# A macaron block on one core: routed experts run unmasked in one stream of tiles, and the choice of experts is multiplied in afterwards

## What is computed

```python
x = x + 0.5 * ffn(layernorm(x))
x = x + attention(layernorm(x))      # 16 heads of 8, 4 key heads, causal, ALiBi bias
x = x + 0.5 * ffn(layernorm(x))

def ffn(x):                           # 8 experts of 64, 2 chosen; one shared of 128
    scores = sigmoid(x @ gate_w.T + lb_bias)
    topw, topi = top_k(scores, 2)
    topw = topw / (topw.sum(-1) + 1e-8)
    for e in range(8):
        sel = (topi == e).any(-1)
        wmean = (topw * (topi == e)).sum() / max((topi == e).sum(), 1)
        y = (silu(x @ gate[e].T) * (x @ up[e].T)) @ down[e].T
        out += where(sel, y * wmean, 0)
    return out + shared_mlp(x)
```

## Time and profile before

| | us |
|---|---|
| median of 3 runs | 787.71 (786.26 to 789.75) |
| the profiled execution | 790.5, span 788.7 |
| PE busy | 733.0 (93% of the span) |
| DVE busy | 579.1 (73%) |
| ACT busy | 420.3 (53%) |
| POOL busy | 42.3 (5%) |
| mean granted TensorE clock | 0.961 |

### The profile page before, as it was taken

The page is one execution under the profiler, slowest core; times in us unless marked ns, Lnnn a source line. Parts: engine busy times, 40 slices in busy tenths (PEclk is TensorE's granted clock), DMA queues, the critical chain, the costliest instruction groups (busy, mean ns, idle before and its releaser), DMA issues.

```text
span 788.7 us, 15244 instructions
## 1 busy us (share of the span) xinstructions
PE 733.0 (93%) x5580; PEld 342.5 (43%) x5588; DVE 579.1 (73%) x1937; ACT 420.3 (53%) x610; POOL 42.3 (5%) x60
## 2 busy tenths in 40 slices
PE   5889998995899999999999999999998878899998
PEld 3634444553334444444444444444343466344443
DVE  5676332889899999999999999999994276643311
ACT  2433343332377776876777677777777523333211
POOL 3200000111000000000000000000000022000000
PEclk9799999996599999999999999999999988999999
DMA  7001000354100110101100110011000000000012
GB/s 204 1 0 16 0 0 1 118 161 137 56 19 24 32 36 21 30 23 36 31 24 19 37 36 19 20 36 36 20 19 1 2 1 1 0 1 0 1 40 67
DMA packets 37983, 26.15 MB, mean 33 GB/s; under 512 B 12026, under 2 KB 37242, under 8 KB 37908
## 3 DMA queue, kind: packets, MB, share of 16 engines
q1 hardware_dynamic: 37332, 25.09, 11.3%
q10 hardware_dynamic: 576, 0.08, 0.1%
HBM read 14.64 MB, written 10.26 MB: 32 GB/s over the span
## 4 chain that ended last, share of the span: by engine, by line
PE 48%; DVE 15%; issue 11%; ACT 2%; another core or an unknown queue 0%; DVEq 0%; ACTq 0%
PE ps L981 44%; DVE mx L866 8%; PE ps L986 4%; DVE mx L859 1%; ACT h_all L586 1%; DVE xn L665 1%; DVE stats L653 1%; DVE h_all L859 1%; DVE h_all L676 1%; DVE wb L886 0%; DVE mm_ L883 0%; DVE mv L657 0%; PE ps L1029 0%; ACT xnT_all L507 0%
## 5 line engine op out<-in xcount | busy, mean ns | idle before, releaser
L586 ACT ACTIVATE h_all<-ps 128x1024 f32<-128x1024 f32 (+3 forms) x384 | 291.2, 811 | 111.9 <-PE ps L981 108.7
L866 DVE TENSOR_REDUCE mx<-ps 128x1 f32<-128x512 f32 (+2 forms) x352 | 223.1, 681 | 10.2 <-PE ps L981 7.4
L981 PE MATMUL ps<-ks,xnT_all 57*128 57x512 bf16 (+3 forms) x768 | 179.2, 336 | 14.1 <-DVE mx L859 6.2
L981 PE MATMUL ps<-h_all,vb 128*32 128x512 f32 (+3 forms) x1536 | 163.9, 500 | 0.6 <-ACT osb L575 0.6
L981 PE MATMUL ps<-xnT_all,ks 59*128 59x512 bf16 (+3 forms) x768 | 158.2, 331 | 3.5 <-ACT h_all L586 3.4
L859 DVE CUSTOM_DVE_ANT_0 h_all<-ps,mask_w 128x384 bf16<-128x384 f32 (+1 forms) x256 | 149.3, 618 | 2.1 <-issue 0.5
L981 PEld LDWEIGHTS ps<-ks,xnT_all 57*128 57x128 bf16 x768 | 56.5, 94 | 144.4 <-DVE mx L859 64.7
L676 DVE TENSOR_TENSOR h_all<-ps,sg 128x512 f32<-128x512 f32 x80 | 54.9, 690 | 82.7 <-PE ps L981 51.4
L981 PE MATMUL ps<-cb 64*128 64x64 bf16 (+3 forms) x1216 | 112.5, 214 | 0.0
L503 ACT ACTIVATE sg<-ps 128x512 f32<-128x512 f32 x80 | 47.6, 597 | 101.3 <-PE ps L981 80.2
L981 PE MATMUL ps<-xnT_all,wg 128*128 128x512 f32 x160 | 88.8, 638 | 1.0 <-ACT sg L503 0.9
(11 more groups left out here) (119 smaller groups left out, 534.3 us busy)
## 6 DMA issues: line engine op xcount, KB each, us to landing
xnT_all<-q_scr SPq DMA_DIRECT2D x64, 96.0 KB
q_scr<-qp SPq DMA_DIRECT2D x8, 384.0 KB
ks<-k_scr SPq DMA_DIRECT2D x64, 48.0 KB
x<-in_x SPq DMA_DIRECT2D x8, 256.0 KB, 6.1
q_scr<-qp SPq DMA_DIRECT2D x8, 256.0 KB
out<-x SPq DMA_DIRECT2D x8, 256.0 KB, 2.3
k_scr<-kp SPq DMA_DIRECT2D x48, 32.0 KB
xnT_all<-bias_scr SPq DMA_DIRECT2D x64, 18.0 KB
```

The source lines that it names most:

```text
L586: act.activation(pr[:, (NSTEP * i + s) % PR_BUFS, p:HPG:SLOTS, lo:HALF], ps[:, b:b + 2, lo:HALF], ACT.Exp)\
L866: dve.tensor_reduce(m, src, AX.X, V.max).then_inc(a_out, 1)
L981: return pe.matmul(o, l, r, start=start, stop=stop, skip_group_check=True)
```

## The change

The routed tiles are no longer masked in the gate. All 40 tiles form one list, `TILE_ORDER`, group by group with the shared one first. Thirteen of them run inside the front (one behind the second turn, two behind each later one), 27 follow without a break. Within the front the logits of a group come one group later. The choice runs on DVE between the products of tiles 13 to 20; ahead of tile 20 PE turns the whole choice (128 tokens x 256 values, 0 or 1, bf16) with two transposes, and ACT copies it to `selT`. SP writes it to DRAM (`store_choice`, two DMAs, waited for) and reads it back for one group at a time (`load_mask`, two DMAs of 256 KB): each expert's row of 512 values goes to the 64 partitions of its hidden units. Two buffers hold these masks. POOL multiplies the routed part of `h_all` of a group with its mask, in place and in two halves of 128x1024 (`mask_hidden`, a semaphore `hm`); `down` waits for both.

In the first feed-forward POOL masks groups 0 to 3, then alternates: `rsqrt` c of the next norm, mask 4 + c, for c from 0 to 3, then `rsqrt` 4 to 7. SP loads masks 0 to 2 behind the choice, 3 to 5 behind the ALiBi rows and ACT's key copies, 6 and 7 behind the first stack. In the second feed-forward POOL masks all groups after its `rsqrt`s, and SP loads masks 6 and 7 among the stores of the output. The totals come ahead of tile 25 and the scaling of `wds` behind it; the slopes stand at tile 27, the eight ALiBi steps at tiles 28 to 35, one to a tile. The operands of the mask matmul (`esel`, `maskT`, `unsel`), their fills on POOL and one constant copy on ACT go away.

```diff
-LATE_SHARED = GROUPS - 4
+
+TILE_ORDER = [(c, i) for c in range(GROUPS) for i in (MT, *range(MT))]
+FRONT = (0, 1, 2, 2, 2, 2, 2, 2)
+FRONT_END = sum(FRONT)
+SEL_AT, TOPS_AT = FRONT_END + 7, FRONT_END + 12
+SLOPES_AT = FRONT_END + 14
+MASK_BUFS, MASK_PARTS = 2, 2
+AHEAD = GROUPS // 2
+
+
+def front_tiles(c):
+
+    return range(sum(FRONT[:c]), sum(FRONT[:c + 1]))
+
...
+            def store_choice(f):
+
+                sp.wait_ge(f.mk, 1)
+                rows = sel_scr.rearrange("e (a t p) -> a t e p", a=2, p=P)
+                for a in range(2):
+                    sp.dma_start(rows[a], selT[:, a, :]).then_inc(f.md, 16)
+                sp.wait_ge(f.md, 16 * 2)
+
+            def load_mask(f, c):
+
+                after(sp, f.hm, MASK_PARTS * (c - MASK_BUFS + 1))
+                rows = sel_scr.rearrange("(m k) n -> k m n", k=2)
+                for k in range(2):
+                    src = rows[k, None, :, c * GN:c * GN + GN].broadcast_to([INTER, MT, GN])
+                    sp.dma_start(expert_mask[c % MASK_BUFS][k * INTER:k * INTER + INTER], src)\
+                        .then_inc(s_mask[c % MASK_BUFS], 16)
+
+            store_choice(f1)
+            for c in range(AHEAD - 1):
+                load_mask(f1, c)
             sp.wait_ge(s_bst, 1)
             sp.dma_start(bias_scr[:, 0:2, :], bias_st[:, 0, None, :].broadcast_to([HEADS, 2, SEQ])).then_inc(s_bdma, 16)
...
+            for c in range(AHEAD - 1, AHEAD + 2):
+                load_mask(f1, c)
             store_parts(0, 0, 0)
             sp.wait_ge(f1.dw0, 16 * STORES)
             load_stack(0, 0, 0, 0)
+            for c in range(AHEAD + 2, GROUPS):
+                load_mask(f1, c)
             store_parts(1, 0, 1)
             sp.wait_ge(f1.dw1, 16 * STORES)
             load_stack(0, 0, 0, 1)
...
+            store_choice(f2)
+            for c in range(GROUPS - 2):
+                load_mask(f2, c)
             od = out.rearrange("(c t p) f -> c p t f", t=GT, p=P)
             for c in range(GROUPS):
+                if c < 2:
+                    load_mask(f2, GROUPS - 2 + c)
                 sp.wait_ge(f2.x, c + 1)
                 sp.dma_start(od[c], xt(c)).then_inc(f2.out, 16)
             sp.wait_ge(f2.out, 16 * GROUPS)
...
+            def mask_hidden(f, n, c):
+
+                uses = (n * GROUPS + c) // MASK_BUFS + 1
+                w = MT // MASK_PARTS
+                for part in range(MASK_PARTS):
+                    tiles = slice(w * part, w * part + w)
+                    pool.wait_ge(f.h, HT * c + 1 + w * part + w)
+                    if part == 0:
+                        pool.wait_ge(s_mask[c % MASK_BUFS], 32 * uses)
+                    pool.tensor_tensor(h_all[:, c, tiles, :], h_all[:, c, tiles, :], expert_mask[c % MASK_BUFS][:, tiles, :],
+                                       ALU.mult).then_inc(f.hm, 1)
+
             over_groups(lambda c, par, first, last: rsqrt(c, par, f1.ve, f1.xn, f1.rs))
             clear_keys()
-            pool.wait_ge(f1.U, HT * GROUPS)
-            over_groups(lambda c, par, first, last: rsqrt(c, par, f1.ve2, f1.xn2, f1.rs2))
+            pool.wait_ge(f1.xn, GROUPS)
+            for c in range(AHEAD):
+                mask_hidden(f1, 0, c)
+            for c in range(AHEAD):
+                rsqrt(c, c % 2, f1.ve2, f1.xn2, f1.rs2)
+                mask_hidden(f1, 0, AHEAD + c)
+            for c in range(AHEAD, GROUPS):
+                rsqrt(c, c % 2, f1.ve2, f1.xn2, f1.rs2)
 
             pool.wait_ge(s_late, 16 * len(late_loads))
...
+            for c in range(GROUPS):
+                mask_hidden(f2, 1, c)
...
+                    for k in front_tiles(c):
+                        silu(k, k % 2)
                     if load_constants and c == GROUPS - 2:
                         constants()
...
-                for c in range(LATE_SHARED, GROUPS):
-                    silu(c, c % 2)
-                mask_T(0, 0)
-                over_groups(routed_tiles)
+                for k in range(FRONT_END, len(TILE_ORDER)):
+                    if k == SEL_AT:
+                        act.wait_ge(f.mT, 1)
+                        act.activation(selT.rearrange("p a n -> p (a n)"), ps[:, 2, 0:P].bitcast(BF16), copy)\
+                           .then_inc(f.mk, 1)
+                    silu(k, k % 2)
...
+                    if not first:
+                        for k in front_tiles(c - 1):
+                            hidden(k)
...
+                def choose():
+                    later = iter(range(FRONT_END, len(TILE_ORDER)))
+
+                    def tile_between():
+                        hidden(next(later))
+
+                    dve.wait_ge(f.sig, 1)
+                    ch.link(dve.tensor_reduce(m1, sc, AX.X, V.max))
+                    ch.link(dve.tensor_tensor(eq, sc, wide(m1), V.is_equal))
                     ch.link(dve.tensor_tensor(eq, eq, rk, V.mult))
-                    ch.link(dve.tensor_reduce(r, eq, AX.X, V.max))
-                    ch.link(dve.tensor_tensor(sel, rk, wide(r), V.is_equal))
-
...
+                    tile_between()
+                    ch.link(dve.tensor_reduce(r1, eq, AX.X, V.max))
+                    ch.link(dve.tensor_tensor(pick1, rk, wide(r1), V.is_equal))
+                    tile_between()
                     ch.link(dve.scalar_tensor_tensor(out=s2, in0=pick1, scalar=-4.0, in1=sc,
                                                      op0=V.mult, op1=V.add))
-                    shared(LATE_SHARED)
-                    shared(LATE_SHARED + 1)
-                    first_max(s2, m2, r2, pick2)
...
+                    ch.link(dve.tensor_reduce(m2, s2, AX.X, V.max))
+                    tile_between()
+                    ch.link(dve.tensor_tensor(eq, s2, wide(m2), V.is_equal))
+                    ch.link(dve.tensor_tensor(eq, eq, rk, V.mult))
+                    tile_between()
+                    ch.link(dve.tensor_reduce(r2, eq, AX.X, V.max))
+                    ch.link(dve.tensor_tensor(pick2, rk, wide(r2), V.is_equal))
+                    tile_between()
+                    dve.tensor_tensor(sel[:, :, :], pick1, pick2, V.add).then_inc(f.sel, 1)
                     dve.tensor_tensor(routed[:, :, 1, :], pick1, pick2, V.add)
                     ch.link(dve.tensor_tensor(den, m1, m2, V.add))
+                    tile_between()
...
+                    tile_between()
                     dve.tensor_tensor(wt, pick1, wide(w1), V.mult)
                     ch.link(dve.tensor_tensor(s2, pick2, wide(w2), V.mult))
+                    tile_between()
                     ch.link(dve.tensor_tensor(routed[:, :, 0, :], wt, s2, V.add))
                     assert ch.n == TOP_LINKS, ch.n
                     dve.tensor_reduce(tot[:, :, :], routed[:, :, :, :].rearrange("p t w e -> p w e t"), AX.X, V.add)\
                        .then_inc(f.tot, 1)
+                    return next(later)
...
                 statistics(0, 0)
                 over_groups(front)
                 finish(GROUPS - 2, 0)
+                for k in front_tiles(GROUPS - 1):
+                    hidden(k)
                 finish(GROUPS - 1, 1)
                 ch.at(LN_LINKS * GROUPS)
-                choose()
-                slopes = slope_parts() if first_ffn else None
-                over_groups(routed_tiles)
+                start = choose()
+                assert SEL_AT < start < TOPS_AT
+                for k in range(start, len(TILE_ORDER)):
+                    hidden(k)
+                    if k == TOPS_AT:
+                        scale_down()
+                    if first_ffn and k == SLOPES_AT:
+                        slopes = slope_parts()
+                    if first_ffn and SLOPES_AT < k <= SLOPES_AT + 8:
+                        bias_rows(slopes, k - SLOPES_AT - 1)
...
+                def up(k):
+                    b = k % 2
+                    c, tile = TILE_ORDER[k]
+                    xT = xnT_all[:, c, :]
                     after(pe, f.sg, k - 1)
-                    mm(bank(3 + b), wg[:, tile, :], xT, stop=False)
+                    mm(bank(3 + b), wg[:, tile, :], xT).then_inc(f.G, 1)
                     after(pe, f.h, k - 1)
                     mm(bank(5 + b), wu[:, tile, :], xT).then_inc(f.U, 1)
 
-                def mask_gate(b, tile, mask):
-                    mm(bank(3 + b), esel[:, tile * P:(tile + 1) * P], mask, start=False).then_inc(f.G, 1)
-
...
+                def logits(c, par):
                     pe.wait_ge(f.xA, c + 1)
                     after(pe, f.lg, c - 1)
...
+                def front(c, par, first, last):
+                    pe.wait_ge(f.xn, c + 1)
+                    after(pe, f.xA, c - 1)
+                    turn(lambda t: xn[:, t, :], 7 * par).then_inc(f.T, 1)
+                    if not first:
+                        logits(c - 1, 1 - par)
+                    if c == 1:
+                        pe.wait_ge(s_w, 16 * len(ffn_loads))
+                    for k in front_tiles(c):
+                        up(k)
+
```

(62 more changed lines are left out.)

92 lines of the change are left out of this document (21 added, 71 removed).

## The result

| | before | after |
|---|---|---|
| median (range) | 788.4 (786.3 to 789.8) | 799.4 (798.0 to 800.7) |
| profiled execution's span | 788.7 | 798.9 |
| ratio to before, 95% interval | | 1.0134 (1.0116 to 1.0152) |
| granted clock, mean | 0.961 | 0.940 |

Forecast were 769.0 us and a range of 752 to 791. The time lies above it, on the other side of no change.

A forecast was written before the change was run, and what follows sets the result against it. PE was taken to bound the kernel: span 788.7 - 41.8 (upper parts) + 0.6 and 6.5 (rsqrt waits) + 14 (POOL beside DVE) + 2 (clock) = 770.0, as a median 769.0 us; range 752 to 791.

The forecast's parts named there:

- PE's stream: Upper parts of both feed-forwards: gapless tiles, 83.7 us (-21.7) in the first, 81.1 (-20.1) in the second, -41.8 together.
- gaps in the stream: Rival 4, front: PE's stream has gaps and only mask matmuls and mask turns, 18.4 us, are gained; 792 us, chance 0.05.
- What a mask costs on POOL: POOL's two products per mask: 2.45 us a half, 4.9 a group, up to twice that if the bf16 operand costs.
- mask work is hidden in the second feed-forward: Second feed-forward: eight masks end at about +60 us, the last down needs its one at +80, so no cost.
- how holds are counted: DVE beside POOL: one half (2.45 us) per burst, twice for scaling, three times for xn, 1.7 for bias rows: 14.
- rival 2: DVE scaling and xn: one operation held per half mask, 39.2 us of holds and 6 for the clock; 798 us, chance 0.13.
- what a hold does to PE: PE's clock after idling: matmuls come back slow, +2 us for this and the other stalls, bounds 1 and 8.
- The loads' landing: Mask loads on SP: a group's load lands 3.2 us after the last issue, near the row that runs alone.
- the bound of 12: Mask loads on SP: upper end of the landing time's range, 2.3 to 12 us.
- The order on POOL: First feed-forward's lower part: rsqrt(3) stands behind mask 6, whose load waits behind SP's stores; group 3's turn +6.5 us.
- SP's stores behind the four extra issues: First feed-forward's lower part: later stores pushed back 2 us, within the same 6.5, so nothing more.
- rival 3: Mask supply: a load takes 12 us or a half mask 5, rsqrt(0) and rsqrt(3) each 8 later; 785 us, chance 0.15.

The follow-up runs named there:

- run 3: Changed kernel with the mask loads left out and POOL multiplying only one of each 512 columns: 751.5 us, ratio 0.9519 to the kernel before.
- run 4: Changed kernel with POOL waiting in both feed-forwards until wd is scaled before it starts mask 0: 782.5 us, ratio 0.9923 to the kernel before.
- run 9: Changed kernel with mask loads reading 256 different rows of an input of ones, not four shared rows; nothing masked: 784.2 us, 0.9927 to before.
- run 5: Changed kernel with rsqrt(3) put ahead of mask 6 and rsqrt(4) ahead of mask 7 on POOL: 791.7 us, ratio 1.0037 to the kernel before.
- run 7: Changed kernel with the edits of run 4, run 5 and run 6 together: 773.0 us, ratio 0.9801 to the kernel before.
- run 6: Changed kernel with POOL waiting for a group's xn before it starts the mask behind that rsqrt: 795.2 us, ratio 1.0078 to the kernel before.
- run 11: Changed kernel with each mask product cut in four instead of two: 790.1 us, ratio 1.0021 to the kernel before.
- run 10: Run 8 with mask 5 also ahead of rsqrt(0), masks 6 and 7 behind rsqrt(0) and rsqrt(1): 760.8 us, ratio 0.9638 to the kernel before.
- run 8: Changed kernel plus run 4's edit, first feed-forward's loads ahead of bias stores, masks 0-4 before rsqrt(0), 5-7 behind rsqrt(0)-(2) after xn: 762.2 us, 0.9666.

## Why the prediction failed, step by step

- **PE's stream: right, 4 us too good.** The windows are gapless at 1.00 to 70 us. Second turn to down is 82.3 in the first feed-forward of run 3 (10.89 to 93.18) where 83.7 stood. In the second it is 84.9 in run 3 (623.45 to 708.30) and 83.0 in run 4 by 81.1. PE is busy throughout; what the forecast sized too small there is the stretch at half clock. It had 4 us of it; in run 3 the granted clock is 0.50 from 623 to 633 us. The rival "gaps in the stream" is out.
- **What a mask costs on POOL: near.** 2.1 us a half where 2.45 stood; no cost of the bf16 operand shows in that. That mask work is hidden in the second feed-forward is right: no PE wait for POOL there.
- **The step that failed most: how holds are counted.** I read the earlier trace rows as one hold for a burst of four, and priced one half per burst. In that row POOL had a single memset left, so the burst could be held only once; it could not tell one hold per burst from one per operation. The runs show one per operation, as long as POOL has products ready: four of the seven scaling operations were held in each feed-forward, beside four halves. Scaling took 7.2 longer in the first feed-forward and 7.6 in the second (8.60 and 9.01 by 1.43) where 2.45 stood for each, and xn 3.7 (4.77 by 1.11) in each of three places where 2.45 stood. This was the mechanism of rival 2, which had 798 us and 0.13.
- **Too small even so: what a hold does to PE.** A hold of 7 us leaves PE idle long enough to come back at half rate (0.66 in 80 to 90, 0.50 in 730 to 740). I gave the clock 2 us in all. In the second feed-forward run 4 shortens the upper part by 9.8 (92.85 to 83.03), of which the idle was 6.60; the other 3.2 are matmuls that ran at the lower rate behind it.
- **The loads' landing: mis-sized.** 3.2 after the last issue stood there, about 4 after the first; it is 8. The rows read or write each DRAM row once; the bound of 12 covered it, the choice "near the one that runs alone" didn't. In run 9, with each row read once from another tensor, it is 4. It reaches PE at rsqrt(0), where the turn's shift is +7.5 against the 3.05 forecast (0.6 and one half), and at rsqrt(3), +14.0 against 8.95. Between them the turn of group 1 adds 5.9, where one half (2.45) stood.
- **The order on POOL: right in kind.** rsqrt(3) behind mask 6, behind SP's stores, is there as described, and run 5 removes it. That was the cost of which I was "surest", and it came out at 14.0 by 8.95 only through the two terms above. What the prediction put at nothing beside it, SP's stores behind the four extra issues, is not nothing once this wait is gone: in the kernel after too the store behind them takes SP 10.0 us (155.91 to 165.95) instead of the 5.3 before, and in runs 5 and 7 ACT and then PE wait for it.
- **The total.** Forecast against measured, in us of span: first upper part with its holds -17.5 by -11.6, lower part +16.5 by +28.9, attention 0 by +1.3, second upper part -17.7 by -8.4. The four differences make 28.9, which is all of 798.9 - 770.0.
- **The rivals.** Rival 2's number, 798, was right, but not its sum: it had 15 and 9.5 for scaling (measured 7.6 and 7.2) and no slow loads. What happened is rivals 2 and 3 together: 25.9 of rival 2's 39.2 us of holds (7.2 + 7.6 + 3 x 3.7), and about half of rival 3's 16 (loads 4 late at two places). I had priced each alone, and a range made of single cases left out the sum of two.

By the Trainium skill's "SBUF — State Buffer", in its section on SBUF's two separate sides, whoever starts first holds the shared port pair for its whole instruction. The trace agrees both ways: DVE's single operations of 2.16 to 2.18 us beside POOL's 2.12, and in run 6 POOL's 4.92 by 4.20 where DVE began first. The sums above go by the rows alone.

What stays open: whether the rows shared by 64 partitions are what lands late, or the tensor that they lie in; why the time through the attention is 1.3 us longer, with masks and without (run 3); and what the clock costs by itself.

## What to carry to other kernels

Work moved to an idle engine is not free when that engine shares a way into memory with the busy one: count each operation of the other engine that falls in the stretch, up to the number of new instructions that stand ready, times one of the new instructions, and ask which of them the bounding engine waits for. Keep such work out of the short serial stretches (run 4: two waits, 16.9 us), or cut it finer (run 11: 9.3 us). Put the loads it needs ahead of stores that are wanted late, and not in front of stores that another engine waits for; keep small operations on the path out from behind it. Together these made 760.8 us of 799.4 with the same work.

## What the runs showed of the hardware

- While POOL runs a queue of products from SBUF, DVE's COPY, CAST and TENSOR_SCALAR operations on SBUF tiles are let in one per POOL instruction. One of 128x128 takes 2.16 us beside 128x1024 products, 1.19 beside 128x512 and 0.2 to 0.3 alone; a CAST of 128x512 takes 2.24 beside them and 0.43 alone (run 10). DVE's products that read PSUM (L734) kept their 0.69.
- Loads of 256 KB to 64 partitions from four shared DRAM rows of 1 KB each landed after 7.4 and 7.9 us (medians; 6.8 to 8.3 in the other runs); from 256 different rows of an input tensor, 3.9 and 4.0.
- Behind two pairs of such loads the eight small stores of a group took SP 10.0 us to issue instead of 5.3 in the kernel before (4.9 in run 8, where no load stands ahead of them; 6.6 in run 9, where the loads land after 4.0).
- After an idle of 6.2 to 6.6 us PE came back with matmuls of 2.07 per pair instead of 1.02; after the 2.27 of run 11's first feed-forward the pair took 1.12. Between these the length alone does not tell: in run 9 it was 1.12 after 2.88 us of idle, and 2.07 after 2.84:

```profile
719.81 2.07 PE L1032 MATMUL ps<-xnT_all,wu 128*128 128x512 f32 x2 [2.84 <-DVE h_all L733]
```
